# Leaf sweeps of a tridiagonal eigensolver: a square and a guard on ScalarE, three products for the new diagonal, two operations elsewhere in the order

## The reference

```
deg = sum(A, axis 0) + sum(A, axis 1) - diagonal(A)
L_norm = deg^-1/2 * (diag(deg) - A) * deg^-1/2          # 64 x 64
_, U = eigh(L_norm)                                     # its eigenvectors
agg = einsum('mn,bnd->bmd', U.T, x)
h = relu(agg @ W1 + b1); out = h @ W2 + b2
x = layernorm(x + einsum('nm,bmd->bnd', U, out))
```

## Time and profile before

| | |
|---|---|
| median of 3 runs | 2172.83 us |
| the profiled execution | 2171.96 us, its span 2170.2 us |
| VectorE busy over the span | 1457.8 us (67%) |
| ScalarE / GpSimd busy over the span | 868.0 us (40%) / 653.2 us (30%) |
| TensorE busy over the span | 1808.6 us (83%) |

### The profile page before, as it was taken

One profiled execution on the slowest core, in us unless ns is written; L12 is line 12 of the kernel. 1 busy time (PEld: TensorE's weight loads), 2 busy tenths in 40 slices (PEclk: granted clock), 3 DMA queues, 4 the chain that ended last, 5 costly groups with the idle time before them and its releaser, 6 DMA issues. The chain is left out here.

```text
span 2170.2 us, 31902 instructions
## 1 busy us (share of the span) xinstructions
PE 1808.6 (83%) x9508; PEld 1524.7 (70%) x9508; DVE 1457.8 (67%) x5806; ACT 868.0 (40%) x1784; POOL 653.2 (30%) x1040
## 2 busy tenths in 40 slices
PE   3454333326999999999999999999999998979997
PEld 2333333314988888888899999888887886857774
DVE  7999999985778555445444444444444777858886
ACT  2333222201344466333333333232332656646664
POOL 0001344402233466333323332413341113521111
PEclk9999766656999999999999999999999999989999
DMA  6000000000111000000000000000010412200111
GB/s 189 2 2 1 1 1 1 1 1 20 59 49 40 20 19 15 10 10 10 5 11 10 10 10 0 20 1 0 0 39 20 165 59 71 97 30 30 40 40 49
DMA packets 44689, 62.70 MB, mean 29 GB/s; under 512 B 13969, under 2 KB 33297, under 8 KB 44433
## 3 DMA queue, kind: packets, MB, share of 16 engines
q1 hardware_dynamic: 43968, 61.08, 8.3%
q10 hardware_dynamic: 592, 0.17, 0.0%
HBM read 36.08 MB, written 25.17 MB: 28 GB/s over the span
## 5 line engine op out<-in xcount | busy, mean ns | idle before, releaser
L2272 ACT ACTIVATE l_gates<-ps,biases 128x512 f32<-128x512 f32 (+1 forms) x504 | 288.9, 635 | 490.6 <-remote 476.2
L2143 PE MATMUL ps<-l_nodes_in,l_even 128*128 128x512 f32 x1392 | 321.4, 391 | 2.6 <-DVE x L1562 1.9
L2143 PEld LDWEIGHTS ps<-l_nodes_in,l_even 128*128 128x128 f32 x1392 | 260.9, 188 | 59.0 <-DVE x L1562 2.7
L2143 PE MATMUL ps<-l_nodes_in,kept 128*128 128x336 f32 (+1 forms) x1280 | 298.0, 350 | 1.9 <-ACT l_gates L2272 1.8
L2369 DVE TENSOR_TENSOR l_gates<-l_gates 128x512 f32<-128x512 f32 (+1 forms) x72 | 50.2, 697 | 343.3 <-ACT l_gates L2272 343.3
L2059 POOL CAST l_nodes_in<-big 128x512 fp32r (+3 forms) x142 | 100.3, 735 | 548.1 <-remote 520.0
L2143 PEld LDWEIGHTS ps<-l_nodes_in,kept 128*128 128x128 f32 x1280 | 229.4, 188 | 27.3 <-issue 4.3
L2143 PE MATMUL ps<-l_state,l_even 128*128 128x512 f32 x960 | 223.3, 392 | 0.0
L2143 PEld LDWEIGHTS ps<-l_state,l_even 128*128 128x128 f32 x960 | 180.4, 188 | 39.7
L2062 POOL TENSOR_TENSOR l_nodes_in<-big,l_nodes_in 128x512 fp32r<-128x512 f32 (+1 forms) x142 | 200.5, 1433 | 5.7
L995 PE MATMUL ps<-w,sw_xT 128*128 128x128 f32 x256 | 60.5, 431 | 129.6 <-ACT sw_xT L859 129.6
(11 more groups left out here) (561 smaller groups left out, 3909.7 us busy)
## 6 DMA issues: line engine op xcount, KB each, us to landing
x<-in_x SPq DMA_DIRECT2D x4, 2048.0 KB, 16.8
residual<-s_x SPq DMA_DIRECT2D x16, 512.0 KB, 2.6
x<-residual SPq DMA_DIRECT2D x16, 512.0 KB, 7.8
normed<-l_raw SPq DMA_DIRECT2D x16, 512.0 KB, 2.6
x<-normed SPq DMA_DIRECT2D x16, 512.0 KB, 3.2
out<-a_y SPq DMA_DIRECT2D x16, 512.0 KB, 2.8
l_raw<-in_L_gnn_W SPq DMA_DIRECT2D x16, 256.0 KB, 2.8
l_raw<-in_L_gnn_W SPq DMA_DIRECT2D x4, 512.0 KB, 3.6
```

The costliest lines, as they stand in the source:

```text
L2143: return pe.matmul(ps[:, 4 * j + gate, 0:n], weight[w_part][:, at:at + 128].bitcast(F32R), src[:, part, k, 0:n].bitcast(F32R), start=start ...
L2272: act.activation(gates[:, j, gate, 0:n], ps[:, 4 * j + gate, 0:n], ACT.Tanh if gate == G else ACT.Sigmoid, bias=bias[:, gate * KD + j:gate ...
```

## The change

- `H2` leaves VectorE: ScalarE computes Square(H), on a new semaphore. `s4` moves from between `ns` and `pre` to behind the sum of neighbours.
- `floor` leaves VectorE: ScalarE computes 1 - act (Identity with scale -1 and a bias of ones). The value TINY for active edges is now added inside the root, as a bias from memory (`tiny`, a new column, set once).
- `ppn`, `ppx`, `GX`, `G` become `pr` = pp * rY, `GX` = pr * act, `G` = pr * node. `up` stands before `G` and `x1`.
- `zp` of the sweep before stands in front of `C3` instead of behind it.
- On GpSimd `shm` moves from behind CZ to behind the product of eb and Y.

The diff (declarations of semaphores and names left out):

```diff
@@ VectorE, front
-                tt(SH[turn % 2][:, 2, :], d[:, 0:n1], d[:, 1:L], ALU.subtract).then_inc(chain[0], mark("H"))
+                tt(SH[turn % 2][:, 2, :], d[:, 0:n1], d[:, 1:L], ALU.subtract).then_inc(h_ready, 1)
...
-                after("H")
-                tt(E["H2"], SH[turn % 2][:, 2, :], SH[turn % 2][:, 2, :], ALU.mult).then_inc(chain[0], mark("H2"))
...
-                after("H2", "ee")
-                stt(E["s4"], E["ee"], 4.0, E["H2"], ALU.mult, ALU.add).then_inc(s4_ready, 1)
...
                 tt(SH[turn % 2][:, 1, :], d[:, 0:n1], d[:, 1:L], ALU.add).then_inc(sum_ready, 1)
+                after("ee")
+                reach(h2_ready, turn)
+                stt(E["s4"], E["ee"], 4.0, E["H2"], ALU.mult, ALU.add).then_inc(s4_ready, 1)
@@ VectorE, middle
-                after("T3a", "T3b")
-                tt(C3[:, :, :, 8:8 + L], T[:, 0, :, :, :], T[:, 1, :, :, :], ALU.add).then_inc(chain[0], mark("C3"))
                 if before:
                     reach(cz_ready, before)
                     scan(V["zp"], CS[:, 1, 0:L], CZ[:, 0, 0:L], 0.0, ALU.mult, ALU.add).then_inc(zp_ready, 1)
+                after("T3a", "T3b")
+                tt(C3[:, :, :, 8:8 + L], T[:, 0, :, :, :], T[:, 1, :, :, :], ALU.add).then_inc(chain[0], mark("C3"))
...
-                reach(act_ready, turn)
-                ts(floor[:, 0, :], act_k, 0.0, TINY, ALU.is_equal, ALU.max).then_inc(chain[0], mark("floor"))
@@ VectorE, end
-                after("pp")
-                tt(V["ppn"], V["pp"], V["node"], ALU.mult).then_inc(chain[0], mark("ppn"))
-                after("pp")
-                tt(E["ppx"], V["pp"][:, 1:L], act_k, ALU.mult).then_inc(chain[0], mark("ppx"))
...
                 reach(ry_ready, turn)
-                after("ppx")
-                tt(E["GX"], E["ppx"], V["rY"][:, 1:L], ALU.mult).then_inc(chain[0], mark("GX"))
+                after("pp")
+                tt(V["pr"], V["pp"], V["rY"], ALU.mult).then_inc(chain[0], mark("pr"))
...
+                after("pr")
+                tt(E["GX"], V["pr"][:, 1:L], act_k, ALU.mult).then_inc(chain[0], mark("GX"))
                 reach(ry_ready, turn)
-                after("ppn")
-                tt(V["G"], V["ppn"], V["rY"], ALU.mult).then_inc(chain[0], mark("G"))
+                tt(E["up"], Yp[:, 2:L + 1], V["rY"][:, 1:L], ALU.mult).then_inc(chain[0], mark("up"))
+                after("pr")
+                tt(V["G"], V["pr"], V["node"], ALU.mult).then_inc(chain[0], mark("G"))
@@ ScalarE
-                act.activation(sq[:, :, :], mx[:, :, :], ACT.Sqrt).then_inc(sq_ready, 1)
+                act.activation(sq[:, :, :], mx[:, :, :], ACT.Sqrt, bias=tiny).then_inc(sq_ready, 1)
...
+                act.wait_ge(h_ready, turn)
+                act.activation(E["H2"], SH[turn % 2][:, 2, :], ACT.Square).then_inc(h2_ready, 1)
                 act.wait_ge(s4_ready, turn)
                 act.activation(E["R"], E["s4"], ACT.Sqrt).then_inc(r_ready, 1)
+                act.wait_ge(act_ready, turn)
+                act.activation(floor[:, 0, :], act_k, ACT.Identity, bias=t["ones"][0:N, 0:1],
+                               scale=-1.0).then_inc(floor_ready, 1)
@@ GpSimd: these lines stood in front of q (L916), with no wait for h_ready
+                reach(tst_ready, turn)
+                reach(sum_ready, turn)
+                reach(h_ready, turn)
+                tt(shm[:, :, :], SH[turn % 2][:, :, :], tst[turn % 2][:, None, :].to_broadcast([N, 3, n1]),
+                   ALU.mult).then_inc(shm_ready, 1)
```

More of the change, by code:

```diff
@@ L519, in sweep_leaves @@
     names = ("ee", "es", "H2", "s4", "R", "dd", "thr", "ns", "pre", "hs", "hsR", "nv", "node", "eb", "dm1", "dm", "dnn", "ad1",
-             "dxx", "ndx", "pp", "N2", "rY", "ppn", "ppx", "GX", "G", "x1", "tst", "nm", "eem", "eY", "up", "down",
+             "dxx", "ndx", "pp", "N2", "rY", "pr", "GX", "G", "x1", "tst", "nm", "eem", "eY", "up", "down",
              "q", "xx", "junk", "zp", "q1", "zero", "flip")
@@ L535, in sweep_leaves @@
     CS, CZ = sb("CS", 2, L + 1), sb("CZ", 2, L + 1)
-    one = sb("one", 2)
-    nsig, active = one[:, 0:1], one[:, 1:2]
+    one = sb("one", 3)
+    nsig, active, tiny = one[:, 0:1], one[:, 1:2], one[:, 2:3]
     flag = ctx.enter_context(nc.sbuf_tensor("sw_count", [1, 1], mybir.dt.int32))
@@ L548, in sweep_leaves @@
         "ry_ready", "rn_ready", "s4_ready", "sg_ready", "sgs_ready", "sha_ready", "shm_ready", "sq_ready",
-        "sum_ready", "ta_ready", "tst_ready", "w_ready", "xx_ready", "z_ready", "zp_ready")
+        "sum_ready", "h_ready", "h2_ready", "floor_ready", "ta_ready", "tst_ready", "w_ready", "xx_ready", "z_ready", "zp_ready")
     (
@@ L552, in sweep_leaves @@
      eb_ready, eby_ready, es_ready, mx_ready, neb_ready, q_ready, q1_ready, ry_ready, rn_ready, s4_ready, sg_ready,
-     sgs_ready, sha_ready, shm_ready, sq_ready, sum_ready, ta_ready, tst_ready, w_ready, xx_ready, z_ready, zp_ready) = every = [sem(s) for s in signals]
+     sgs_ready, sha_ready, shm_ready, sq_ready, sum_ready, h_ready, h2_ready, floor_ready, ta_ready, tst_ready, w_ready, xx_ready, z_ready, zp_ready) = every = [sem(s) for s in signals]
     act_met, pool_met, act_go, pool_go, begun_ready, pool_done, active_ready, total_ready, flag_ready, flag_used = (
@@ L596, in begin @@
                                  (V["pre"], 1.0), (V["zero"], 0.0), (V["ee"], 0.0), (SA[:, :, :], 0.0),
-                                 (SH[0][:, 0, :], 1.0), (SH[1][:, 0, :], 1.0), (floor[:, 1, :], TINY), (sgn[:, 0, :], 0.25), (CS[:, 0, :], 1.0),
+                                 (SH[0][:, 0, :], 1.0), (SH[1][:, 0, :], 1.0), (floor[:, 1, :], TINY), (tiny, TINY), (sgn[:, 0, :], 0.25), (CS[:, 0, :], 1.0),
                                  (CS[:, 1, :], 0.0), (CZ[:, :, :], 0.0), (Pp[:, 0:1], 1.0), (Yp[:, 0:1], 1.0),
@@ L743, in sweep @@
                 stt(sgn[:, 1, :], E["q"], -1.0, E["es"], ALU.mult, ALU.mult).then_inc(sgs_ready, 1)
+                after("pr")
+                tt(E["GX"], V["pr"][:, 1:L], act_k, ALU.mult).then_inc(chain[0], mark("GX"))
                 reach(ry_ready, turn)
-                after("ppn")
-                tt(V["G"], V["ppn"], V["rY"], ALU.mult).then_inc(chain[0], mark("G"))
+                tt(E["up"], Yp[:, 2:L + 1], V["rY"][:, 1:L], ALU.mult).then_inc(chain[0], mark("up"))
+                after("pr")
+                tt(V["G"], V["pr"], V["node"], ALU.mult).then_inc(chain[0], mark("G"))
                 after("GX", "ndx")
                 tt(V["x1"], V["GX"], V["ndx"], ALU.add).then_inc(chain[0], mark("x1"))
-                reach(ry_ready, turn)
-                tt(E["up"], Yp[:, 2:L + 1], V["rY"][:, 1:L], ALU.mult).then_inc(chain[0], mark("up"))
                 reach(ry_ready, turn)
@@ L756, in sweep @@
                 reach(cs2_ready, turn)
-                after("floor")
+                reach(floor_ready, turn)
                 tt(mx[:, :, :], cs2[:, :, :], floor[:, :, :], ALU.max).then_inc(mx_ready, 1)
@@ L910, in sweep @@
                        ALU.mult).then_inc(cz_ready, 1)
[L911 to L914, removed]
                 reach(sg_ready, turn)
```

## The result

The changed kernel takes 2178.8 us (median of 8 runs, 2176.57 to 2180.44) against 2173.04 for the kernel before in the same runs: ratio 1.0028, 95% interval [1.0019, 1.0037], some 6 us slower. The profiled execution took 2176.57 us, at the fast end of its own runs. The prediction was 2175.8, in a range of 2168 to 2180: the time lies inside the range, but beyond the 0.2% that the likeliest case allowed.

The account below looks back on a forecast made before the run. VectorE's chain of dependent operations was taken to set the sweeps' pace: front +0.07, middle -0.06, end +0.08 make +0.09 us per sweep, 2.9 over 32, plus 0.1 once, added to the 2172.83 median: about 2175.8 us, range 2168 to 2180.

Parts of the forecast that it names:

- the likeliest case: Whole kernel: the forecast of about 2175.8 us, chance 0.52, with about 0.2% (4.3 us) taken as what a measurement can tell.
- Operations that ride in a wait save nothing when removed: VectorE in the sweep: H2 between thr and ns, floor between P and its square; distances stay 0.20 us, saving 0.
- Rival 1: Sweep on VectorE: each operation costs its place, three fewer save 0.29 us per sweep, 9 us, giving 2163.6; chance 0.14.
- Front: Sweep start: sum, s4 and act crowd behind pre, so act and everything behind come about 0.07 us later.
- Middle: T3a to C3: with shm gone from there, T3a takes 0.21 us and C3 comes 0.06 us earlier per sweep.
- End: Yp to the next sweep: three products save nothing; moved shm delays pr, costing 0.05 to 0.12 us, taken as 0.08.
- Rival 2: Sweep end: GpSimd's moved product catches two critical operations, pr and the sign; +0.14 us per sweep, 2177.3 to 2179; chance 0.19.
- Rival 3: Sweep end: shm catches nothing; +0.01 us per sweep, 0.3 us in all, 2173.1; chance 0.11.
- Rival 4: Something unstated: table loads adding 82 us, or 16 more sweeps from changed rounding, over 107 us; chance 0.04.
- The sum: Front, middle and end together: +0.09 us per sweep, 2.9 us over 32 sweeps, plus 0.1 once for the longer last root.
- the step from the sweep to the kernel: Sweep loop to end: merges need the sweeps' result, so each sweep's gain or loss passes on whole, 32 times.
- the slow side: Whole kernel: a result slower than the forecast by more than about 0.2% (4.3 us); chance 0.28.

Follow-up runs that it names:

- e8_scalar_only: Kernel before with only the square and the guard moved to ScalarE (H2, s4, floor, bias tiny), 64 VectorE instructions a sweep; ratio 1.0023.
- e4_three_products: Kernel before with only the three products for four and up's new place, 64 VectorE instructions a sweep; ratio 0.9999.
- e3_sum_first: Changed kernel with the sum of neighbours between ns and pre, and s4 in the sum's old place; ratio 1.0021 against the kernel before.
- e5_one_wait: Kernel before with one satisfied VectorE wait added per sweep ahead of ns, 66 instructions a sweep; ratio 0.9998.
- f_66: Changed kernel with three harmless VectorE waits per sweep, the third before act, 66 instructions; 2178.34 us, ratio 1.0026 against the kernel before.
- e1_two_waits: Changed kernel with two satisfied waits per sweep between thr and ns, which became one instruction (64 a sweep); ratio 1.0028 against the kernel before.
- e6_riders: Changed kernel with sum, sign, mx, up, Square moved, and shm behind CZ waiting for T3a; 2164.26 us, ratio 0.9970 against the kernel before.
- f_63: Changed kernel as it is, 63 VectorE instructions a sweep, rerun in the one-chip comparison; 2179.46 us, ratio 1.0029 against the kernel before.
- f_64: Changed kernel with one harmless VectorE wait per sweep, 64 instructions, same one-chip comparison; 2179.03 us, ratio 1.0027 against the kernel before.
- f_65: Changed kernel with two harmless VectorE waits per sweep, 65 instructions, same one-chip comparison; 2174.99 us, ratio 1.0010 against the kernel before.

## Why the prediction was right, and what it missed

- *Operations that ride in a wait save nothing when removed*: right. thr to ns and P to its square kept their 0.20; e8_scalar_only and e4_three_products, each with fewer operations, have a sweep of 6.77 and 6.75 us, not under 6.72. Rival 1 (each operation costs its place, 2163.6) is refuted.
- *Front, +0.07*: right in kind, +0.05 in size (the median over the sweeps). The sum is followed after 0.07, not 0.10, by s4. e3_sum_first shows that the crowding behind pre is the whole of it. R came in time: hsR starts 0.35 behind act, as before.
- *Middle, -0.06*: right, -0.07; taking shm away did it, the scan's place nothing.
- *End, +0.05 to +0.12*: right, +0.09: 0.08 from shm's catching pr, 0.02 from a longer way from the reciprocal to its first user, for which I had counted nothing. Rival 2's second catch did not come: the sign starts at 438.65, GpSimd's next at 438.66, by the margin of 0.01 us. The measured 2178.8 lies in that rival's 2177.3 to 2179, but by the stops and not by its mechanism. Rival 3 (shm catches nothing) is refuted by pr's 0.23. Rival 4 did not come: no table load and no further sweep.
- *The sum*, +0.09 a sweep and 3.0 us: measured +0.08 and 2.5 us.
- *What failed is the step from the sweep to the kernel*: "what a sweep gains or loses passes to the end whole, 32 times" held, but I took the ordinary sweep for all sweeps and for all that depends on the count of instructions. The stops marked "issue" at L723 (0.2 us) and behind the tests (2.02 us) could be read in the trace of the kernel before; they were left out of the sum. They brought 1.0 and 2.4 us, more than the operations. So the likeliest case's "within 0.2%" was wrong and the time fell on the slow side, to which 0.28 had been given. That the time still lies in the range is luck in part: the range was drawn for terms of the operations, and more than half of the loss came from outside them.

What stays open: that the stops have to do with the fetching of code is inferred from the count of 128 and from the packets of the instruction queue, not shown by a change of theirs alone; why one boundary in a busy stretch costs 0.35 us and another nothing; why e5_one_wait, with 66 a sweep, lost nothing in the median; and why there are two long stops behind the tests with 63 instructions (four kernels) and in f_66, but only one with 64 and 65 and in e5_one_wait.

## What to carry to other kernels

On an engine that runs small dependent operations, write down the starts, not the durations: an operation in the shadow of a wait is free, so removing one is worth nothing and moving one into such a place is worth all of its place. Before an operation moves to another engine, see what will run on VectorE and GpSimd at the same time. And when unrolled code changes by a few instructions, compare the ordinary pace and the stops apart: here the same arithmetic moved by 4 us with two harmless waits.

## What the runs showed of the hardware that I had not expected

- VectorE lost 0.12 to 0.35 us at instructions number 63 to 65 modulo 128 of its stream in some places (five in the kernel before, nine in the changed one) and nothing in others, places in a busy stretch among them. With 64 instructions a sweep the same operation was met 15 times: at a cost of 0.25 us in e1_two_waits and 0.18 in e8_scalar_only, at none in e4_three_products and e6_riders.
- An 8 KB packet of the instruction queue starts within 1 us of each of these places, where time was lost mostly 0.6 to 0.7 us after the late operation.
- After the sweeps a second stop of 1.9 to 2.2 us came or went with the number of instructions before it (f_63 and f_66 have it, f_64 and f_65 not). Every long stop there ended 1.7 to 2.0 us after the start of such a packet.
- Two waits on one semaphore in one place became one instruction.
